# One clamp pass instead of two in a quantised feed-forward, with the scale handed to the gelu

## The chip, the cores and the metric

The kernel runs on one core of a Trainium2 chip. The metric is the device time of one execution in microseconds (us), lower is better. Five engines work beside each other, each with its own queue of instructions: TensorE (PE) for matmuls, VectorE (DVE), ScalarE (ACT), GpSimd (POOL) and SyncE (SP), which here only issues DMA transfers. They meet at semaphores: an instruction may wait for a count and raise one when it is done.

## The reference, cut to what matters

The model is a stack of small layers over 4096 tokens of 96 channels (16 images of 16 x 16): two convolution-like attention layers, a causal attention, a quantised feed-forward, a second causal attention and a mixture of four experts. The change is in the quantised feed-forward alone:

```
def _quantize_activations_groupwise(x):
    for g in range(NUM_GROUPS):                      # 5 groups along the batch
        ag = x[g * gs:(g + 1) * gs]
        gamma = jnp.max(jnp.abs(ag))
        xq[g] = clip(ag * QB / (gamma + EPS), -QB + EPS, QB - EPS)
def _bitlinear(x, W, b):
    y = einsum('btc,oc->bto', x, sign_binarised(W)) + b
    return _quantize_activations_groupwise(y)
h = _bitlinear(x, W1, b1)                            # 96 -> 384
h = jax.nn.gelu(h, approximate=False)
out = _bitlinear(h, W2, b2)                          # 384 -> 96
```

QB is 128 and EPS is 1e-5. Each group has one gamma, the largest magnitude over all its 768 tokens and all channels.

## The kernel before, in words

The layers run one after another on the one core, and nearly everything stays in SBUF. The order of every engine's work in this feed-forward is written by hand in three lists of steps (lines 76 to 78), one an engine. The digit of a step is its group of 768 tokens:

- TensorE, `F2_PE`: "h" is the first projection of a group, six pairs of matmuls into six PSUM buffers (L1035); "y" is the second projection, in two halves of 36 matmul records together (L1048).
- ScalarE, `F2_ACT`: "c" copies the six results of a group from PSUM into `big` (L652); "e" is the gelu of a whole group, in place (L656), 128 partitions by 3 x 768 elements. The gelu's activation table is loaded once, ahead of e0.
- VectorE, `F2_DVE`: "a" takes each partition's largest magnitude of a group (L1406); "q" quantises the group in place; "y" adds the bias to the second projection and takes its maximum (L1419, L1422); "f" quantises that, adds it to the residual and takes the token statistics (L1427, L1428, L1146, L1149).
- GpSimd makes the maximum over partitions of each "a" and "y" (L425).

So the lists begin on VectorE with a0, a1, q0, a2, q1, a3, q2, y0, a4, q3, y1, f0, q4, y2, f1, y3, and on TensorE with h0, h1, h2, h3, y0, h4, y1. On ScalarE the order is c0, c1, c2, e0, c3, e1, c4, e2, e3, e4. The second projection of group g starts when gelu g is done and VectorE has read the same half of the projection before. The third maximum and the later ones wait for the copies of their own group.

A step "q" starts with `quant_scale`: three one-column operations (L1398, L1399, L1400), each linked to the one before by a semaphore. They put gamma + EPS into column 2k+1 of `amax` and the scale QB / (gamma + EPS) into column 2k, the same number on all partitions. Then come two passes over the group: L1411 multiplies by the scale (a per-partition operand) and takes the minimum with a constant, L1412 takes the maximum with a constant. The gelu waits for the second.

After the feed-forward VectorE goes on to the layer norm (L1157 to L1165), whose output TensorE transposes (L706) for the next attention.

Of the kernel before, what the change touches and what calls it, by code (L numbers as in the profile page):

```python
# [9 lines left out]
ALU = mybir.AluOpType  # L10
ACT = mybir.ActivationFunctionType
# [5 lines left out]
P = 128  # L17
# [9 lines left out]
NG = 5  # L27
GI = B // NG
GT = GI * N
NE = 4  # L30
QB = 128.0
QEPS = 1e-5
# [52 lines left out]
def hybrid_kernel(nc, x_d, w96_d, w128_d, out_d):  # L85
    ctx = ExitStack()
    with ctx:
        def sb(name, shape, dt=F32):
            return ctx.enter_context(nc.sbuf_tensor(name, shape, dt))
# [3 lines left out]
        def sg(name):  # L93
            if name not in sems:
                sems[name] = ctx.enter_context(nc.semaphore(name))
            return sems[name]
# [59 lines left out]
        def wa(name, rows=P):  # L156
            a, b = C96[name]
            return w96[0:rows, a:b]

        def wb(name, rows=P):  # L160
            a, b = C128[name]
            return w128[0:rows, a:b]
# [31 lines left out]
        y1 = big[:, :].rearrange("p (j t) -> p j t", j=NJ)  # L194
# [11 lines left out]
        qk_f = qk[:, :, :, :, :].rearrange("p a h b x -> p (a h b x)")  # L206
        xhl = qk_f[:, 0:2048].rearrange("p (a b t) -> p a b t", a=2, b=2)
        amax = sb("amax", [P, 4, NG])
        gate = sb("gate", [P, 2, NT, NE])
        cmp = sb("cmp", [P, 6, NT])  # L210
        gsel = sb("gsel", [P, NE, NT])
# [231 lines left out]
        def _(act):  # L443
# [7 lines left out]
            def norm_tail(name):  # L451

                norm_sqrt(name, P, NT)
                act.wait_ge(sg("norm_scale"), TURN[name] // 8 + 1)
                for g in range(9):
                    if g < 8:
                        t = 4 * g + 3
                        nc.scalar.activation(on[:, t, :], tok[:, t, :], ACT.Identity, bias=st[:, 6, t:t + 1],
                                             scale=st[:, 5, t:t + 1]).then_inc(sg("ln_ta"), 1)
                    if g >= 1:  # L460
                        act.wait_ge(sg("ln_t_ps"), TURN[name] + g)
                        nc.scalar.activation(xn[0:C, (g - 1) * 512:g * 512], ps[0:C, 4 + (g - 1) % 4, :], ACT.Copy).then_inc(sg("xn_copied"), 1)
# [108 lines left out]
            for l in (1, 2, 3):  # L571
# [61 lines left out]
                if l == 2:  # L633

                    act.wait_ge(sg("f2_z"), 1)
                    for g in range(NG):
                        n = HID // NG
                        nc.scalar.activation(wa("f2_w1", C)[:, g * n:(g + 1) * n], wa("f2_w1", C)[:, g * n:(g + 1) * n], ACT.Sign,
                                             bias=s64[:, 1, g:g + 1]).then_inc(sg("f2_w1s"), 1)
                    for g in range(NG):  # L640
                        n = C // NG
                        v = wb("f2_w2").rearrange("p (j o) -> p j o", j=NJ)[:, :, g * n:(g + 1) * n]
                        nc.scalar.activation(v, v, ACT.Sign, bias=amax[:, 3, g:g + 1]).then_inc(sg("f2_w2s"), 1)
                    norm_tail("lnf2")
                    act.sem_inc(sg("f2_y1"), 6)
                    for step in F2_ACT:
                        g = int(step[1])
                        if step[0] == "c":
                            for b in range(2):
                                for j in range(NJ):  # L650
                                    act.wait_ge(sg("f2_y1_ps"), g * 6 + (b * NJ + j + 1))
                                    nc.scalar.activation(y1[:, j, g * GT + b * (GT // 2):g * GT + (b + 1) * (GT // 2)], ps[:, b * NJ + j, 0:GT // 2],  # L652
                                                         ACT.Copy).then_inc(sg("f2_y1"), 1)
                        else:
                            act.wait_ge(sg("f2_quant"), g + 1)
                            nc.scalar.activation(y1[:, :, g * GT:(g + 1) * GT], y1[:, :, g * GT:(g + 1) * GT], ACT.Gelu).then_inc(sg("f2_gelu"), 1)  # L656
            for g in range(8):
                act.wait_ge(sg("xres_ps"), g + 1)
                nc.scalar.activation(xc[:, g * 512:(g + 1) * 512], ps[0:C, g % 4, :], ACT.Copy).then_inc(sg("xres"), 1)
# [445 lines left out]
        def _(dve):  # L1105
# [3 lines left out]
            V = nc.vector  # L1109
            chain = [0]  # L1110

            def link(ins):

                chain[0] += 1
                ins.then_inc(sg("dve_chain"), 1)
                dve.wait_ge(sg("dve_chain"), chain[0])
# [176 lines left out]
            for l in (1, 2, 3):  # L1293
# [83 lines left out]
                if l == 2:  # L1377

                    n1, n2 = HID // NG, C // NG
                    V.tensor_reduce(out=s64[:, 0, 0:NG], in_=wa("f2_w1", C)[:, 0:NG * n1].rearrange("p (g o) -> p g o", g=NG), axis=AX.X, op=ALU.add).then_inc(sg("f2_wsum"), 1)  # L1380
                    w2v = wb("f2_w2").rearrange("p (j o) -> p j o", j=NJ)
                    for j in range(NJ):
                        last = V.tensor_reduce(out=cmp[:, j, 0:NG], in_=w2v[:, j, 0:NG * n2].rearrange("p (g o) -> p g o", g=NG), axis=AX.X, op=ALU.add)
                    link(last)
                    V.tensor_reduce(out=amax[:, 2, :], in_=cmp[:, 0:NJ, 0:NG].rearrange("p j g -> p g j"), axis=AX.X, op=ALU.add).then_inc(sg("f2_wsum"), 1)
                    dve.wait_ge(sg("f2_wtot"), 1)
                    V.tensor_scalar(s64[:, 1, 0:NG], ps[0:C, 0, 0:NG], -1.0 / (n1 * C), None, ALU.mult)
                    V.tensor_scalar(amax[:, 3, :], ps[:, 1, 0:NG], -1.0 / (n2 * HID), None, ALU.mult).then_inc(sg("f2_z"), 1)

                    V.memset(wa("f2_w1", C)[:, NG * n1:HID], 0.0).then_inc(sg("f2_w1z"), 1)  # L1390
                    V.memset(w2v[:, :, NG * n2:C], 0.0).then_inc(sg("f2_w2z"), 1)
                    layer_norm("lnf2")

                    def quant_scale(k, g):

                        dve.wait_ge(sg(f"f2_gmax{k}"), g + 1)
                        m, q = amax[:, 2 * k + 1, g:g + 1], amax[:, 2 * k, g:g + 1]
                        link(V.tensor_scalar(m, m, QEPS, None, ALU.add))  # L1398
                        link(V.reciprocal(q, m))  # L1399
                        link(V.tensor_scalar(q, q, QB, None, ALU.mult))  # L1400

                    for step in F2_DVE:
                        what, g = step[0], int(step[1])
                        if what == "a":
                            dve.wait_ge(sg("f2_y1"), g * 6 + 12)
                            V.tensor_reduce(out=amax[:, 0, g:g + 1], in_=y1[:, :, g * GT:(g + 1) * GT], axis=AX.XY, op=ALU.max,  # L1406
                                            apply_absolute_value=True).then_inc(sg("f2_amax0"), 1)
                        elif what == "q":
                            quant_scale(0, g)
                            v = y1[:, :, g * GT:(g + 1) * GT]  # L1410
                            link(V.tensor_scalar(v, v, amax[:, 0, g:g + 1], QB - QEPS, ALU.mult, ALU.min))  # L1411
                            V.tensor_scalar(v, v, -QB + QEPS, None, ALU.max).then_inc(sg("f2_quant"), 1)  # L1412
                        elif what == "y":
                            if g == 0:
                                dve.wait_ge(sg("f2_w2s"), NG)
                            for b in range(2):
                                dve.wait_ge(sg("f2_y2_ps"), 2 * g + b + 1)
                                t0 = g * 6 + b * 3
                                V.tensor_tensor(y2[:, t0:t0 + 3, :], ps[:, 6 + b, 0:3 * C].rearrange("p (t c) -> p t c", c=C),  # L1419
                                                mid_dim(wb("f2_b2"), 1, 3), ALU.add).then_inc(sg("f2_y2"), 1)  # L1420
                            dve.wait_ge(sg("f2_y2"), 2 * g + 2)
                            V.tensor_reduce(out=amax[:, 2, g:g + 1], in_=y2[:, g * 6:(g + 1) * 6, :], axis=AX.XY, op=ALU.max,  # L1422
                                            apply_absolute_value=True).then_inc(sg("f2_amax1"), 1)
                        else:
                            quant_scale(1, g)
                            v, tv = y2[:, g * 6:(g + 1) * 6, :], tok[:, g * 6:(g + 1) * 6, :]
                            link(V.tensor_scalar(v, v, amax[:, 2, g:g + 1], QB - QEPS, ALU.mult, ALU.min))  # L1427
                            link(V.scalar_tensor_tensor(out=tv, in0=v, scalar=-QB + QEPS, in1=tv, op0=ALU.max, op1=ALU.add))  # L1428
                            link(token_stats(range(6 * g, 6 * g + 6 if g < NG - 1 else NT)))
# [131 lines left out]
```

## Time and profile before

| | us |
|---|---|
| median of three runs | 922.02 |
| lowest and highest | 921.21 and 923.03 |
| profiled execution | 921.3 |
| its span, first to last instruction | 919.5 |
| TensorE busy | 796.1 (87%) |
| VectorE busy | 613.9 (67%) |
| ScalarE busy | 573.9 (62%) |
| GpSimd busy | 231.2 (25%) |

The mean granted clock of TensorE over the span is 0.923 of full speed. The feed-forward's work on the groups lies between some 509 and 574 us of the span. The busy shares are averages over stages with different limits, so they don't tell which engine bounds one stage: that is read from the chain that ended last, which is followed back from the last instruction to whatever released each step, and from the timelines of the stage. A row of a timeline merges equal instructions that follow each other; the bracket at its end is how long the engine was idle before it, and who released it.

### The profile page before, as it was taken

How to read it: one execution, taken by the hardware profiler on the slowest of the kernel's cores; microseconds unless marked ns; L12 is line 12 of the kernel's file. 1: busy time of each engine (PE TensorE's matmuls, PEld its weight loads, DVE VectorE, ACT ScalarE, POOL GpSimd, SP SyncE). 2: the span in 40 equal slices, each digit the busy share in tenths (PEclk: the TensorE clock that was granted, in tenths of full speed). 3: DMA queues.
4: the chain of work that ended last, by engine and by line, in shares of the span. 5: the costliest groups of instructions: out<-in, count | busy, mean ns of one | idle time of the engine just before them, and what ended most of it. 6: DMA issues, size and time to landing. Idle time of an engine off the chain costs nothing.

```text
span 919.5 us, 17419 instructions
## 1 busy us (share of the span) xinstructions
PE 796.1 (87%) x5452; PEld 606.3 (66%) x5452; DVE 613.9 (67%) x1584; ACT 573.9 (62%) x1341; POOL 231.2 (25%) x443
## 2 busy tenths in 40 slices
PE   0866799999999889999993874489999978999997
PEld 0852477878777867777772564257777758777775
DVE  6325677676668255777777599367677773677876
ACT  0202377777777356878884731467888754788875
POOL 9000336655553560000000000200000000234344
PEclk9998699999999698999996987789999985999999
DMA  5000001011111122333330000133333310231230
GB/s 191 1 0 1 0 2 14 16 17 18 18 19 18 26 70 71 99 89 86 103 94 9 1 1 0 44 88 86 92 103 87 87 33 3 69 86 44 57 74 17
DMA packets 63267, 44.42 MB, mean 48 GB/s; under 512 B 34416, under 2 KB 55280, under 8 KB 63088
## 3 DMA queue, kind: packets, MB, share of 16 engines
q1 hardware_dynamic: 63216, 43.78, 18.7%
q8 instruction: 27, 0.44, 0.2%
q14 instruction: 24, 0.20, 0.1%
HBM read 12.24 MB, written 3.21 MB: 17 GB/s over the span
## 4 chain that ended last, share of the span: by engine, by line
PE 75%; DVE 14%; issue 3%; ACT 2%; DMA 2%; POOL 2%; SPq 2%; POOLq 0%; DVEq 0%; ACTq 0%
PE ps L933 12%; PE ps L772 9%; PE ps L835 9%; PE ps L1085 7%; PE ps L1074 7%; PE ps L779 5%; PE ps L783 3%; PE ps L791 3%; PE ps L792 2%; PE ps L804 2%; PE ps L813 2%; DVE xn L1140 2%; DVE chst L1146 2%; PE ps L827 2%; SPq L242 2%
## 5 line engine op out<-in xcount | busy, mean ns | idle before, releaser
L502 ACT ACTIVATE ee<-ps,nmax 128x128 f32<-128x128 f32 (+1 forms) x584 | 207.9, 445 | 12.7 <-DVE nmax L1226 9.0
L933 PE MATMUL ps<-w,ee 128*128 128x128 f32 x960 | 140.9, 275 | 3.1 <-ACT big L489 0.9
L1226 DVE TENSOR_REDUCE nmax<-ps 128x2 f32<-128x256 f32 x200 | 101.8, 551 | 52.9 <-PE ps L783 52.9
L933 PEld LDWEIGHTS ps<-w,ee 128*128 128x128 f32 x960 | 111.6, 142 | 24.3 <-ACT ee L502 8.9
L489 ACT ACTIVATE big<-ps 128x512 f32<-128x512 f32 (+1 forms) x192 | 99.2, 546 | 24.6 <-PE ps L933 20.5
L1488 DVE TENSOR_TENSOR hhl<-ee,hhl 128x512 fp32r<-128x512 f32 x96 | 79.8, 837 | 32.2 <-ACT hhl L680 30.6
L1223 DVE TENSOR_REDUCE nmax<-ps 128x4 f32<-128x1024 f32 x48 | 58.8, 1225 | 58.8 <-PE ps L772 58.8
L772 PE MATMUL ps<-kh,big 128*128 128x256 f32 x384 | 93.8, 388 | 1.2 <-ACT ee L502 1.2
L835 PE MATMUL ps<-big,vh 128*32 128x256 f32 (+1 forms) x1188 | 92.2, 353 | 0.0
L306 POOL COPY xb<-xn 96x256 f32 (+1 forms) x52 | 20.6, 399 | 277.0 <-PE ps L804 248.1
L436 POOL TENSOR_TENSOR xc<-big,xc 96x512 f32<-96x512 f32 x32 | 52.6, 1643 | 135.9 <-DVE big L1482 135.7
L1074 PE MATMUL ps<-qk,w1hl 128*128 128x512 f32 x288 | 85.1, 407 | 0.4 <-DVE ee L1491 0.4
L1085 PE MATMUL ps<-hhl,w2hl 128*96 128x512 f32 x288 | 83.5, 399 | 0.3 <-DVE hhl L1488 0.3
L772 PEld LDWEIGHTS ps<-kh,big 128*128 128x128 f32 x384 | 71.4, 193 | 16.9 <-ACT ee L502 6.9
L1320 DVE COPY big<-ps 128x384 f32<-128x384 f32 x96 | 52.8, 550 | 38.8 <-PE ps L933 38.8
L677 ACT ACTIVATE ee<-ps 128x512 f32<-128x512 f32 x96 | 57.7, 601 | 30.5 <-PE ps L1074 30.5
L312 POOL TENSOR_TENSOR big<-qs,w 96x256 f32<-96x256 f32 x96 | 55.8, 613 | 70.6 <-ACT qs L511 70.6
L1341 DVE BATCH_NORM_STATS2 est<-ee 128x6 f32<-128x256 f32 x192 | 66.9, 411 | 0.0
L1074 PEld LDWEIGHTS ps<-qk,w1hl 128*128 128x128 f32 x288 | 55.9, 195 | 16.6 <-DVE ee L1491 0.7
L835 PEld LDWEIGHTS ps<-big,vh 128*32 128x32 f32 x1188 | 39.9, 110 | 39.9 <-issue 21.8
L779 PE MATMUL ps<-qk 64*128 64x128 f32 (+1 forms) x400 | 50.7, 332 | 10.7 <-DMA qk<-hl 7.7
L1085 PEld LDWEIGHTS ps<-hhl,w2hl 128*96 128x96 f32 x288 | 47.0, 164 | 18.9 <-issue 1.3
(241 smaller groups left out, 1339.0 us busy)
## 6 DMA issues: line engine op xcount, KB each, us to landing
qk<-hl SPq DMA_DIRECT2D x288, 96.0 KB, 3.1
big<-moe_gate SPq DMA_DIRECT2D x8, 768.0 KB, 6.7
w<-w_in SPq DMA_DIRECT2D x1, 1735.5 KB, 12.6
xc<-x_in SPq DMA_DIRECT2D x4, 384.0 KB, 5.6
l_mix<-on SPq DMA_DIRECT2D x32, 48.0 KB, 2.0
tok<-l_mix SPq DMA_DIRECT2D x16, 96.0 KB, 2.0
out<-xc SPq DMA_DIRECT2D x8, 192.0 KB, 2.1
w<-w_in SPq DMA_DIRECT2D x1, 998.0 KB, 9.0
```

What stands on the lines that cost most here:

```text
L489: nc.scalar.activation(et[:, h, 0:w], ps[:, 4 + hh, 0:w], ACT.Copy).then_inc(own(l, f"et{hh}"), 1)
L502: last = nc.scalar.activation(ee[:, ke, hh, qc, 0:w], src, ACT.Exp, bias=nmax[:, kp, hh, qc:qc + 1])
L772: last = mm(ps[:, 2 * kp + hh, qc * N:(qc + 1) * N], qh[:, par, 2 * u + hh, qc * P:(qc + 1) * P], kh[:, par, :], start=True, stop=True)
L779: mm(ps[:, 2 * kp + hh, qc * N:qc * N + w], qk[r0:r0 + 4 * HD, par, u, 0, qc * P:(qc + 1) * P], qk[r0:r0 + 4 * HD, par, u, 1, 0:w], start= ...
L835: last = mm(ps[32 * r:32 * (r + 1), 6, g * N + q0:(g + 1) * N], vh[:, par, tc, 3 * g + r, :], et[:, 3 * g + r, tc * N:tc * N + N - q0], st ...
L933: last = nc.tensor.transpose(ps[:, 4 + hh, b * P:(b + 1) * P], ee[:, u, hh, qc, tc * P:(tc + 1) * P], ident)
L1074: last = mm(ps[:, 4 + n % 4, :], w1hl[:, w, s * P:(s + 1) * P], xhl[:, t % 2, x, :], start=(k == 0), stop=(k == 2))
L1085: last = mm(ps[0:C, e, :], w2hl[:, w, s * C:(s + 1) * C], hhl[:, n % 4, h, :], start=(j == 0 and k == 0), stop=(j == NJ - 1 and k == 2))
L1223: last = V.tensor_reduce(out=nmax[:, kp, :, :].rearrange("p h q -> p (h q)"), in_=src, axis=AX.X, op=ALU.max, negate=True)
L1226: last = V.tensor_reduce(out=nmax[:, kp, :, qc], in_=ps[:, 2 * kp:2 * kp + 2, qc * N:qc * N + scores_cols(l, qc)], axis=AX.X, op=ALU.max, ...
L1341: last = V.bn_stats(est[:, par, q, 2 * u + hh, :], ee[:, u, hh, q, :])
L1488: V.tensor_tensor(hhl[:, n % 4, 1, :], hf[:, n % 4, :], hhl[:, n % 4, 0, :].bitcast(F32), ALU.subtract).then_inc(sg("moe_lo"), 1)
```

## The change

The clamp of step "q" becomes one pass. Clamping v times s to plus or minus (QB - EPS) is the same as clamping v to that bound divided by s, and multiplying afterwards. Since s is QB / (gamma + EPS), the bound on v is (gamma + EPS) (QB - EPS) / QB, which is computed in `amax`'s column 1 by a one-column multiplication; a second one writes its negative into a new one-column tile `bound`. The one large pass then takes the minimum with the first and the maximum with the second, both as per-partition operands. The multiplication by s moves into the gelu of ScalarE, which takes s as its per-partition scale operand. The two small operations are linked by the semaphore, as the three before them are.

```
@@ buffers
         amax = sb("amax", [P, 4, NG])
+        bound = sb("bound", [P, NG])
@@ ScalarE, step e
                             act.wait_ge(sg("f2_quant"), g + 1)
-                            nc.scalar.activation(y1[:, :, g * GT:(g + 1) * GT], y1[:, :, g * GT:(g + 1) * GT], ACT.Gelu).then_inc(sg("f2_gelu"), 1)
+                            nc.scalar.activation(y1[:, :, g * GT:(g + 1) * GT], y1[:, :, g * GT:(g + 1) * GT], ACT.Gelu,
+                                                 scale=amax[:, 0, g:g + 1]).then_inc(sg("f2_gelu"), 1)
@@ VectorE, step q
                             quant_scale(0, g)
+                            top, low = amax[:, 1, g:g + 1], bound[:, g:g + 1]
+                            link(V.tensor_scalar(top, top, (QB - QEPS) / QB, None, ALU.mult))
+                            link(V.tensor_scalar(low, top, -1.0, None, ALU.mult))
                             v = y1[:, :, g * GT:(g + 1) * GT]
-                            link(V.tensor_scalar(v, v, amax[:, 0, g:g + 1], QB - QEPS, ALU.mult, ALU.min))
-                            V.tensor_scalar(v, v, -QB + QEPS, None, ALU.max).then_inc(sg("f2_quant"), 1)
+                            V.tensor_scalar(v, v, top, low, ALU.min, ALU.max).then_inc(sg("f2_quant"), 1)
```

VectorE's order before, from the first two maxima through step q0 to the third maximum (`big` holds the group, 3 x 768 elements a partition; the bracket names the semaphore waited for):

```order
433 L1406 TENSOR_REDUCE amax<-big 128x1 [waits f2_y1] x2
434 L1398 TENSOR_SCALAR amax<-amax 128x1 [waits f2_gmax0]
435 L1399 RECIPROCAL amax<-amax 128x1 [waits dve_chain]
436 L1400 TENSOR_SCALAR amax<-amax 128x1 [waits dve_chain]
437 L1411 TENSOR_SCALAR big<-big,amax 128x3x768 [waits dve_chain]
438 L1412 TENSOR_SCALAR big<-big 128x3x768 [waits dve_chain]
439 L1406 TENSOR_REDUCE amax<-big 128x1 [waits f2_y1]
```

The same place now (lines stand two lower on VectorE and one lower on ScalarE):

```order
433 L1408 TENSOR_REDUCE amax<-big 128x1 [waits f2_y1] x2
434 L1400 TENSOR_SCALAR amax<-amax 128x1 [waits f2_gmax0]
435 L1401 RECIPROCAL amax<-amax 128x1 [waits dve_chain]
436 L1402 TENSOR_SCALAR amax<-amax 128x1 [waits dve_chain]
437 L1413 TENSOR_SCALAR amax<-amax 128x1 [waits dve_chain]
438 L1414 TENSOR_SCALAR bound<-amax 128x1 [waits dve_chain]
439 L1416 TENSOR_SCALAR big<-big,amax,bound 128x3x768 [waits dve_chain]
440 L1408 TENSOR_REDUCE amax<-big 128x1 [waits f2_y1]
```

Two one-column operations stand where the first large pass stood, the second large pass has two operands more, and nothing else has moved. On ScalarE the order stays; this is its piece around the first gelu now:

```order
368 L653 ACTIVATE big<-ps 128x384 [waits f2_y1_ps] x18
369 L657 ACT_TABLE_LOAD
370 L657 ACTIVATE big<-big,amax 128x3x768 [waits f2_quant]
371 L653 ACTIVATE big<-ps 128x384 [waits f2_y1_ps] x6
372 L657 ACTIVATE big<-big,amax 128x3x768 [waits f2_quant]
373 L653 ACTIVATE big<-ps 128x384 [waits f2_y1_ps] x6
```

Only the operand `amax` has come to the gelu.

## Rows read from the trace of the kernel before

**Rows 1.** The page: the chain that ended last, by engine, share of span.

```profile
PE 75%; DVE 14%; issue 3%; ACT 2%; DMA 2%; POOL 2%; SPq 2%; POOLq 0%; DVEq 0%; ACTq 0%
```

**Rows 2.** The chain, 490 to 600 us: start us, us, what.

```profile
555.00 5.87 PE ps L1048 x36
...
560.89 0.47 DVE on L1419
```

**Rows 3.** Waits, 505 to 575 us: waiting <- awaited: us in total, times, longest.

```profile
ACT big L656 <- DVE big L1412: 18.8, 5, 7.0
...
DVE on L1419 <- PE ps L1048: 1.0, 1, 1.0
```

**Rows 4.** Timeline of VectorE, 505 to 580 us: start us, us, instruction, idle before.

```profile
517.53 2.55 DVE L1406 TENSOR_REDUCE amax<-big 128x1 f32<-128x2304 f32 x1 [1.32 <-ACT big L652]
520.00 0.14 DVE L1398 TENSOR_SCALAR amax<-amax 128x1 f32<-128x1 f32 x1
520.18 0.16 DVE L1399 RECIPROCAL amax<-amax 128x1 f32<-128x1 f32 x1
520.38 0.15 DVE L1400 TENSOR_SCALAR amax<-amax 128x1 f32<-128x1 f32 x1
520.57 1.82 DVE L1411 TENSOR_SCALAR big<-big,amax 128x2304 f32<-128x2304 f32 x1
522.42 1.76 DVE L1412 TENSOR_SCALAR big<-big 128x2304 f32<-128x2304 f32 x1
524.10 2.54 DVE L1406 TENSOR_REDUCE amax<-big 128x1 f32<-128x2304 f32 x1
...
527.11 1.82 DVE L1411 TENSOR_SCALAR big<-big,amax 128x2304 f32<-128x2304 f32 x1
...
537.19 0.81 DVE L1419 TENSOR_TENSOR on<-ps,w 128x288 f32<-128x288 f32 x2
...
545.25 0.81 DVE L1419 TENSOR_TENSOR on<-ps,w 128x288 f32<-128x288 f32 x2
...
554.41 0.81 DVE L1419 TENSOR_TENSOR on<-ps,w 128x288 f32<-128x288 f32 x2
```

**Rows 5.** Timeline of ScalarE in the same stretch.

```profile
521.39 1.28 ACT L656 ACT_TABLE_LOAD   x1
524.21 2.12 ACT L656 ACTIVATE big<-big 128x2304 f32<-128x2304 f32 x1 [1.54 <-DVE big L1412]
526.24 2.38 ACT L652 ACTIVATE big<-ps 128x384 f32<-128x384 f32 x6
...
532.79 2.38 ACT L652 ACTIVATE big<-ps 128x384 f32<-128x384 f32 x6
```

**Rows 6.** Timeline of TensorE there; below, its busy us and granted clock (PEclk).

```profile
526.48 4.23 PE L1048 MATMUL ps<-w,big 128*128 128x96 f32 x36 [1.77 <-ACT big L656]
530.55 4.06 PE L1035 MATMUL ps<-xn,w 128*128 128x384 f32 x12
537.77 5.86 PE L1048 MATMUL ps<-w,big 128*128 128x96 f32 x36 [3.16 <-DVE on L1419]
...
540.00:542.00 2.00, 2.00 (x11) 0.50 0.00 0
```

**Rows 7.** Lines L1307, L1140, L1165, L458: ns min/median/max, starts, forms.

```profile
L1307 DVE TENSOR_SCALAR w<-w x2: 200/206/211, 101.1 to 581.5; 128x96 f32<-128x96 f32 x2
...
L1140 DVE TENSOR_SCALAR xn<-xc,st x32: 394/404/4109, 15.0 to 98.3; 96x256 f32<-96x256 f32 x32
...
L1165 DVE TENSOR_SCALAR on<-tok,st x72: 320/325/334, 499.0 to 758.2; 128x96 f32<-128x96 f32 x72
...
L458 ACT ACTIVATE on<-tok,st x24: 450/454/467, 499.0 to 765.6; 128x96 f32<-128x96 f32 x24
```

**Rows 8.** Timeline of ScalarE, 750 to 785 us, at another table load.

```profile
774.16 1.28 ACT L677 ACT_TABLE_LOAD   x1
775.45 0.60 ACT L677 ACTIVATE ee<-ps 128x512 f32<-128x512 f32 x1
```

## The prediction

> **What bounds the kernel now.** I read the chain that ended last first, then the waits of the stretch that the change touches, then its timelines engine by engine. Over the whole span the chain lies on TensorE for 75% and on VectorE for 14% [rows 1], so most of the 919.5 us can't gain from an edit of VectorE. In the quantised feed-forward it is the other way round. From 517.5 us, where the second maximum (step a1) stops waiting for ScalarE, the chain runs through VectorE alone until 555 us, where it goes once to TensorE and comes back at 560.89 [rows 2]. The waits say the same: ScalarE waits 18.8 us for the clamp's last pass, and VectorE waits for TensorE only once, 1.0 us, ahead of an L1419 [rows 3]. So what leaves VectorE between 520 and 554 us leaves the span, as long as nobody else comes late. After 554 us the order of work is unchanged and moves as one block: VectorE feeds the last two projections, then the statistics, then the layer norm, on which everything later waits.
>
> **The block that changes.** One step "q" on VectorE is three linked one-column operations (start to start 0.18, 0.20 and 0.19 us), then L1411 (1.82 us, multiply by the scale and clamp above), then L1412 (1.76 us, clamp below). L1411 starts at 520.57, L1412 at 522.42, and the next maximum at 524.10 [rows 4]: 3.53 us from the first large pass to the next step. There are five such steps, one a group.
>
> *Removed:* both large passes, 3.53 us a step.
>
> *Added, the one large pass.* It reads two per-partition bounds; no row has that form at this size. What a per-partition operand costs: L1307, 128x96 with a constant alone, takes 206 ns; L1165, the same shape with two per-partition operands, 325 ns [rows 7]. So two of them cost 119 ns. L1411 has one and takes 61 ns more than L1412, which fits. That the two don't slow the rate is seen between 96 and 256 columns: 325 and 404 ns, 0.49 ns a column [rows 7], no more than the 0.76 of L1412 (1758 ns for 2304). So I take 1.76 + 0.12 = 1.88 us. The next maximum needs no result of it and starts before it has ended: 524.10 against the end of L1412 at 522.42 + 1.76 = 524.18, an overlap of 0.08. Start to start: 1.80 us. The low end would be one operand's price, as L1411's 1.82 (1.74 start to start). The high end is the rate of the maximum over the same elements, 2.54 us [rows 4], plus 0.12: 2.66, or 2.58 start to start. I take 1.80, since the shape and pass are those of L1412 and both two-operand rows lie on the fast side.
>
> *Added, two one-column operations*, each waiting for the one before. They are of the kind of L1398 and L1400, 0.18 to 0.20 start to start [rows 4]; 0.37 together, and nothing hides them, as they are ahead of the large pass. Between 0.30 (their own durations with nothing between) and 0.40.
>
> Saved a step: 3.53 - 1.80 - 0.37 = 1.36 us; five steps: **6.8 us**. The ends: with 1.74 and 0.36, 1.43 a step, 7.1; with 2.58, 0.58 a step, 2.9.
>
> *Added, the scale on the gelu.* ScalarE reads one per-partition operand more. L458, 96 columns with two of them, takes 454 ns [rows 7]; at the gelu's 2.12 us for 2304 columns [rows 5] 96 of them are at most 0.09, so an operand costs between nothing and 0.18 us. I take 0.1, the middle: the gelu becomes 2.22 us, between 2.12 and 2.30. It is paid beside VectorE's work. The cover is checked next.
>
> **Does everybody else keep up?** I walk the new times. q0: its three small operations are at 520.00 as before; the pass starts at 520.57 + 0.37 = 520.94 and ends at 522.82.
> - *Gelu 0.* The activation table is loaded from 521.39 to 522.67 [rows 5], so it is ready 0.15 us before the data. The gelu starts at 522.85 (before: 524.21) and ends at 525.07. The six copies of group 3 took 2.38 us and started 0.09 before the gelu's end [rows 5]; now they end at about 527.4. The maximum a3 wants them when VectorE has done q1: a2 starts at 522.74, its q1 pass 3.01 + 0.37 later (524.10 to 527.11 before [rows 4]) at 526.12, a3 at 527.92. Cover 0.5 us.
> - *Projection 0 and the matmuls of group 4.* They followed the gelu by 0.15 us and lasted until 534.61 [rows 6]; now 1.26 earlier, 533.35, and the last copy of group 4 is done half a microsecond behind, at about 533.9 (ScalarE, with gelu 1 done at 530.2, has caught up by then). VectorE reaches y0 at 537.19 - 3 x 1.36 = 533.10 and a4 1.51 us later (8.06 between y0 and y1, less 3.02 and 3.53), 534.6. Cover 0.7.
> - *Projection 1* began 0.58 after y0 and took 5.86 us [rows 4, 6]: from 533.7 to 539.5. VectorE takes its first half at 545.25 - 4 x 1.36 = 539.8. Its cover shrinks from 1.6 to 0.3, and the half read first is done well before.
> - *Projection 2* starts behind y1's first half, at 540.4, and is done at 546.2; y2 is reached at 554.41 - 6.8 = 547.6. Cover 1.4. From there all is as before, the 1.0 us wait too.
>
> TensorE's clock matters here. Projection 0 took 4.23 us with the clock granted in full (2.4 GHz); projection 1, at 0.50 (1.2 GHz) for a part (540 to 542 [rows 6]), took 5.86 after a pause. One such stretch is worth 1.63 us. In y3 (5.87 us, also one stretch) it is what makes VectorE wait: without it 1.0 us more is gained, with a second one 1.6 lost. The change moves the work against these stretches, and I can't tell which way: it goes into the range.
>
> Here a rule of the Trainium skill speaks against the change. The row first: behind the table load of 774.16, 1.28 us long, the activation starts at 775.45, 0.01 us after its end [rows 8]; behind the one at 521.39 nothing shows it, because the gelu waits for VectorE until 524.21 anyway. The skill's page "ScalarE: Activation LUTs", section "What ACT_TABLE_LOAD costs", gives a switch of tables a drain of about 1.38 us beside the 1.28 us load. If that stood behind the load, the sum would be 6.1 instead of 6.8 (an estimate from that figure, by the way of rival 2); by the row it is 6.8, and I go by the row.
>
> **The sum.** The profiled execution took 921.3 us (919.5 in the span, 1.8 around it); less 6.8 is 914.5. The median of the runs is 922.02, 0.7 above it, so the predicted time is 922.0 - 6.8 = 915.2.
>
> **Rivals.**
> 1. *The two-bound pass runs one element at a time*, at the maximum's rate. 2.9 us saved: 919.1. For: no row has the form at 3 x 768. Against: the two-operand rows of 96 and 256 columns. 8%.
> 2. *ScalarE becomes the bound at group 3.* If the first gelu can't start sooner than it did, at 524.21, because ScalarE needs until then after its table load, it ends at 526.4, the copies of group 3 at 528.7, and a3 waits 0.8 us (528.7 against 527.9). Projection 0 and the copies of group 4 then end where they did, 535.2, against a4 at 535.4: they just hold. 6.0 saved: 916.0. The skill's section on the table load speaks for it. For: only 0.15 us between load and data. Against: the activation at 775.45 [rows 8]. 10%.
> 3. *Slower.* The clamp with both bounds taken from operands is issued as two turns over the elements, each at the maximum's rate: 5.1 us, 5.0 start to start. Then a step costs 5.0 + 0.37 - 3.53 = 1.84 more, 9.2 in all: 931.2. It turns slower once the pass is over 3.16 us start to start (3.53 - 0.37), 1.4 ns an element. For: minimum and maximum with two operands stand in no row. Against: L1411 and L1412 have the same rate whatever they compute. 3%.
> 4. *No change*: the gain is taken back by TensorE, as stretches at the lower clock in the layer norms and attentions that follow. It would take four stretches of 1.63 more than before, and rows show no reason why they should all fall on one side. 3%.
>
> **How the numbers follow.** My forecast has 76%, with a range of its own of 913.2 to 917.8: 7.8 or 7.1 saved at one end and 5.2 (a second stretch) at the other, and a microsecond around the median, as the three runs lie between 921.21 and 923.03. For 8 in 10 I give 912.8 to 918.4, which takes in rival 2 and leaves out rivals 1, 3 and 4. About 0.2% (1.8 us) is what a measurement of this kernel can tell from no change: faster 76 + 10 + 8 = 94, less 1 for rival 1's 919.1 lying near that bound: 93%; the same 3 + 1 = 4%; slower 3%.
>
> **What the profile after would show.** One large pass of about 1.88 us, five of them, and the next maximum 1.80 us after its start; two more one-column operations, 0.37 us a step. Large pass to next maximum and back: 5.2 us instead of 6.54 in the first three groups. Gelus of 2.2 us, the first starting at 522.85. VectorE idle between the first maximum and the layer norm still about 1 us, in y3 alone. The second half of y3 6.8 us earlier than 560.89. A pass of 2.6 us or more, a gelu starting at 524, a wait of the fourth maximum for ScalarE, or a wait at y1 for TensorE would each show a step wrong.

## The result, and the profile after

| | us | ratio to before, 95% |
|---|---|---|
| before, median | 922.27 | |
| changed kernel, median of four runs (913.94 to 915.72) | 915.15 | 0.9922 (0.9905 to 0.9939) |
| predicted | 915.2 | |

7.1 us faster, where 6.8 were forecast. Timed again beside the experiments, the changed kernel took 915.74, a ratio of 0.9929 (0.9917 to 0.9942).

The timeline of VectorE after, over step q0 and into the third maximum, has these rows (start us, us, instruction, idle before); lines stand two lower than before:

```profile
519.78 2.55 DVE L1408 TENSOR_REDUCE amax<-big 128x1 f32<-128x2304 f32 x1 [1.32 <-ACT big L653]
522.25 0.14 DVE L1400 TENSOR_SCALAR amax<-amax 128x1 f32<-128x1 f32 x1
...
522.62 0.15 DVE L1402 TENSOR_SCALAR amax<-amax 128x1 f32<-128x1 f32 x1
522.81 0.15 DVE L1413 TENSOR_SCALAR amax<-amax 128x1 f32<-128x1 f32 x1
523.00 0.15 DVE L1414 TENSOR_SCALAR bound<-amax 128x1 f32<-128x1 f32 x1
523.19 1.88 DVE L1416 TENSOR_SCALAR big<-big,amax,bound 128x2304 f32<-128x2304 f32 x1
524.99 2.54 DVE L1408 TENSOR_REDUCE amax<-big 128x1 f32<-128x2304 f32 x1
...
528.38 1.88 DVE L1416 TENSOR_SCALAR big<-big,amax,bound 128x2304 f32<-128x2304 f32 x1
...
556.36 0.46 DVE L1423 TENSOR_TENSOR on<-ps,w 128x288 f32<-128x288 f32 x1 [0.96 <-PE ps L1050]
...
570.15 0.18 DVE L1159 TENSOR_SCALAR st<-chmv 128x32 f32<-128x32 f32 x1
```

Beside [rows 4]: the pass takes 1.88 us and the next maximum starts 1.80 after it (3.53 before for the two), the two new operations take 0.19 each, and from pass to pass it is 5.19 us instead of 6.54. The last row is the layer norm's first operation behind the feed-forward. In the timeline of before it is this one:

```profile
574.68 0.18 DVE L1157 TENSOR_SCALAR st<-chmv 128x32 f32<-128x32 f32 x1
```

I use the distance from the second maximum to this row as the length of the stretch. It is 57.15 us before (517.53 to 574.68) and 50.37 after (519.78 to 570.15): 6.78 us less. That is the forecast, instruction by instruction. From here on "the stretch" is this distance, and "the rest" is the span without it.

The span fell by 5.6 us (919.5 to 913.9), not by 6.8, because the rest of the kernel, which is untouched, differs between executions: 2.25 us more ahead of the stretch, 1.07 less behind it. About 0.6 us of the first arises between 80 and 112 us of the span, where TensorE's clock was lower. These are the windows of TensorE's busy us (with its instructions) and granted clock, first before, then after:

```profile
80.00:108.00 28.00, 14.26 (x38) 0.63 0.00 1
```

```profile
80.00:108.00 28.00, 14.23 (x34) 0.57 0.00 1
```

In the executions before, after and in c0, e1, e2, e3, e6, e8, e9 and e10 the rest took between 861.5 and 865.0 us, with nearly nothing edited there. So one execution's span can't show a microsecond. The stretch can, as it came out at 50.37 or 50.38 in the three executions in which its work was the same (after, c0, e10); but it too moves by a microsecond or two when TensorE's lower clock falls on another of its matmuls, as e4 shows below, so it has to be read with its waits.

Who waits for whom in the stretch after (505 to 570 us):

```profile
ACT big L657 <- DVE big L1416: 10.4, 4, 5.6
...
DVE on L1423 <- PE ps L1050: 1.0, 1, 1.0
...
PE ps L1050 <- ACT big L657: 0.5, 1, 0.5
```

Beside [rows 3]: ScalarE's wait for VectorE fell from 18.8 to 10.4 us, and VectorE still waits only for the one half of projection 3. The chain that ended last crosses to TensorE at the same place as in [rows 2]:

```profile
550.46 5.87 PE ps L1050 x36
```

ScalarE after, to be read beside [rows 5]:

```profile
523.63 1.28 ACT L657 ACT_TABLE_LOAD   x1
525.10 2.22 ACT L657 ACTIVATE big<-big,amax 128x2304 f32<-128x2304 f32 x1 [0.19 <-DVE big L1416]
527.23 2.37 ACT L653 ACTIVATE big<-ps 128x384 f32<-128x384 f32 x6
```

The gelu went from 2.12 to 2.22 us by its scale operand. It waited 0.19 us for the data behind the table load, so the load did not delay it. The copies of group 3 end at 529.60, 0.58 ahead of the maximum a3 at 530.18: such a lead of a result over the instruction that asks for it is called its cover here.

TensorE after, beside [rows 6]:

```profile
531.53 4.06 PE L1037 MATMUL ps<-xn,w 128*128 128x384 f32 x12
535.95 4.23 PE L1050 MATMUL ps<-w,big 128*128 128x96 f32 x36 [0.36 <-DVE on L1423]
```

Projection 1 now begins 0.36 us behind the matmuls of group 4 instead of 3.16, its clock stays granted in full, and it takes 4.23 us instead of 5.86; so does projection 2 (at 542.66, before at 545.84). The 1.63 us are worth nothing in either place: projection 1 is done at 540.18, and VectorE reads it after step q3, at 542.07; projection 2 is done at 546.89 and read at 549.87.

### The profile page after: what moved, and what is told of

Its sections match the earlier page's. It is cut to its first block, busy times and chain, and to the rows that moved or that the text cites. A ratio compares the mean times of both kernels' runs of the same rounds, so it can differ in the third digit from the quotient of the medians.

```text
span 913.9 us, 17424 instructions
## 1 busy us (share of the span) xinstructions
PE 794.6 (87%) x5452; PEld 604.3 (66%) x5452; DVE 607.7 (66%) x1589; ACT 575.0 (63%) x1341; POOL 230.4 (25%) x443
## 3 DMA queue, kind: packets, MB, share of 16 engines
q1 hardware_dynamic: 63216, 43.78, 18.8%
## 4 chain that ended last, share of the span: by engine, by line
PE 77%; DVE 14%; issue 3%; ACT 2%; POOL 2%; DMA 2%; SPq 1%; POOLq 0%; DVEq 0%; ACTq 0%
PE ps L935 12%; PE ps L774 9%; PE ps L837 9%; PE ps L1087 7%; PE ps L1076 7%; PE ps L781 5%; PE ps L785 4%; PE ps L793 3%; PE ps L794 2%; PE ps L806 2%; PE ps L815 2%; DVE xn L1142 2%; DVE chst L1148 2%; PE ps L829 2%; PE ps L729 1%
```

## The experiments

The stretch is the one defined above, in the one profiled execution of each kernel. Each ratio is to the kernel before as timed beside that experiment, with its 95% interval.

| kernel | median us | ratio to before, 95% | stretch us |
|---|---|---|---|
| before | 922.3 | | 57.15 |
| c0, changed kernel again | 915.74 | 0.9929 (0.9917 to 0.9942) | 50.38 |
| e1, two passes with the two bounds | 926.40 | 1.0037 (1.0025 to 1.0050) | 60.53 |
| e2, pass over even halves | 914.84 | 0.9914 (0.9901 to 0.9927) | 47.64 |
| e3, small operations side by side | 912.47 | 0.9893 (0.9878 to 0.9908) | 47.01 |
| e4, early table, one run | 920.54 | | 51.98 |
| e5, e2 + e3 + e4 | 915.98 | 0.9937 (0.9919 to 0.9955) | 46.23 |
| e6, idle copy ahead of gelu 0 | 918.38 | 0.9964 (0.9951 to 0.9977) | 53.76 |
| e7, e5 in a new order | 917.69 | 0.9954 (0.9938 to 0.9969) | 50.49 |
| e8, e2 + e3, table behind the hand-over | 910.96 | 0.9884 (0.9866 to 0.9901) | 46.22 |
| e9, e2 + e3 | 912.70 | 0.9897 (0.9882 to 0.9913) | 46.79 |
| e10, the changed kernel with the table load as in e8, one run | 913.67 | | 50.37 |

### c0 and e1: is it the second pass, and nothing else?

> The changed kernel once more, as the mark for the other three. Every theory: 915.2 us, the ratio to the kernel before at 0.992 to 0.993.

> As the changed kernel (bounds made by two small operations, scale in the gelu), but the minimum and the maximum in two large passes again, each with one per-partition bound. My theory (the gain is the length of one pass on VectorE's chain, nothing else): passes of 1.82 us, 1.85 + 1.74 from the first pass to the next step in place of 1.80, so 1.79 x 5 = 9.0 us more than the changed kernel, 924.1 us, 0.2% slower than the kernel before, since the two small operations are then paid for nothing. Rival (the gain comes from taking the multiplication away from VectorE, or from the new times at which TensorE works): 915 to 918 us.

```diff
-    V.tensor_scalar(v, v, top, low, ALU.min, ALU.max).then_inc(sg("f2_quant"), 1)
+    link(V.tensor_scalar(v, v, top, None, ALU.min))
+    V.tensor_scalar(v, v, low, None, ALU.max).then_inc(sg("f2_quant"), 1)
```

926.4 us, slower than the kernel before by 0.25 to 0.50%. VectorE's groups in the stretch (busy us, mean ns, idle before):

```profile
L1424 DVE TENSOR_TENSOR on<-ps,w 128x288 f32<-128x288 f32 x10 | 4.2, 448 | 2.2 <-PE ps L1050 2.1
...
L1417 DVE TENSOR_SCALAR big<-big,bound 128x2304 f32<-128x2304 f32 x5 | 9.1, 1819 | 0.2
L1416 DVE TENSOR_SCALAR big<-big,amax 128x2304 f32<-128x2304 f32 x5 | 9.1, 1818 | 0.2
```

The stretch is 10.15 us longer than in c0: 9.0 for the passes, as expected, and 1.2 because the wait for projection 3 grew from 0.97 to 2.15. The time missed the expected one by 2.3 us: 1.2 is that wait, and in the profiled execution the rest was 1.7 longer than in c0. The rival, that the gain came with the multiplication's move to ScalarE, is refuted: that move is in this kernel, and the gain isn't. Against the kernel before the stretch is 3.4 us longer: 1.9 for the small operations, 0.3 for the operand that the second pass has more, and 1.2 of the wait.

### e2: what sets the rate of the pass?

> As the changed kernel, but the one large pass goes over the same 2304 elements as 2 x 3 x 384 instead of 3 x 768. Theory A (two elements at a time are had only when the outer dimension can be halved, and three rows are run as two turns of 768: 1877 ns is 277 of fixed cost and 1600 for 1536): the pass takes 1.48 us, 0.40 less. Five of them would be 2.0 us; ScalarE's table load ends only 0.19 us before the first gelu, so the copies of group 4 come late by some 0.2 to 0.3 and 1.7 us are saved: 913.4 us. Theory B (the rate of 0.7 ns an element is that of the memory, whatever the shape): 915.2 us, the pass 1.88 us as before. A loss (a pass of 2.6 us, 918.8) if a three-dimensional pattern goes one element at a time.

```diff
+    v = v.rearrange("p j (h t) -> p h j t", h=2)
     V.tensor_scalar(v, v, top, low, ALU.min, ALU.max).then_inc(sg("f2_quant"), 1)
```

The line of the pass in e2 (ns min/median/max, starts, forms):

```profile
L1417 DVE TENSOR_SCALAR big<-big,amax,bound x5: 1478/1478/1480, 523.7 to 547.3; 128x2304 f32<-128x2304 f32 x5
```

1478 ns, the 1.48 us of theory A, for the same elements at the same addresses. Theory B is refuted. The stretch fell by 2.74 us, 1 more than expected: 5 x 0.40, and the wait for projection 3 (1.0) is gone because TensorE's low-clock part fell on projection 2 (5.86 us) instead, less 0.3 of new waits ahead of a3 and a4. That last microsecond is no merit of the pass. The medians differ by 0.9 us (1.7 expected) and the intervals overlap: the time alone would not have decided it.

Behind the table load, with no wait left, the gelu starts at once:

```profile
524.13 1.28 ACT L657 ACT_TABLE_LOAD   x1
525.42 2.22 ACT L657 ACTIVATE big<-big,amax 128x2304 f32<-128x2304 f32 x1
```

### e3: what do five one-column operations cost?

> As the changed kernel, but each step q makes (gamma + eps) / QB and both bounds straight from gamma in three small operations that don't wait for each other, and the reciprocal stands behind them beside the large pass: four small operations with one exposed wait instead of five with five. Step f gets two linked small operations instead of three. Theory (a linked one-column operation costs 0.19 us for the wait on its result, an unlinked one about 0.07): a step q shorter by about 0.5 us and a step f by 0.19, 2.5 + 0.95 = 3.4 us, less some 0.5 of new waits of the maxima a3 and a4 for ScalarE's copies: 912.2 us. Rival (the cost is that of the instruction, not of the link): only one operation less in q and one in f, 0.19 x 10 = 1.9 us, 913.3 us.

```diff
+    V.tensor_scalar(unit, m, QEPS, 1.0 / QB, ALU.add, ALU.mult)
+    V.tensor_scalar(top, m, QEPS, (QB - QEPS) / QB, ALU.add, ALU.mult)
+    link(V.tensor_scalar(low, m, QEPS, (QEPS - QB) / QB, ALU.add, ALU.mult))
+    V.reciprocal(q, unit)
     V.tensor_scalar(v, v, top, low, ALU.min, ALU.max).then_inc(sg("f2_quant"), 1)
```

VectorE's timeline of e3 in q0 and at the two maxima:

```profile
521.45 0.14 DVE L1413 TENSOR_SCALAR bound<-amax 128x1 f32<-128x1 f32 x1
521.51 0.14 DVE L1414 TENSOR_SCALAR bound<-amax 128x1 f32<-128x1 f32 x1
521.57 0.14 DVE L1415 TENSOR_SCALAR bound<-amax 128x1 f32<-128x1 f32 x1
521.75 0.16 DVE L1416 RECIPROCAL amax<-bound 128x1 f32<-128x1 f32 x1
521.83 1.86 DVE L1418 TENSOR_SCALAR big<-big,bound 128x2304 f32<-128x2304 f32 x1
...
528.65 2.55 DVE L1407 TENSOR_REDUCE amax<-big 128x1 f32<-128x2304 f32 x1 [0.35 <-ACT big L653]
...
535.17 2.55 DVE L1407 TENSOR_REDUCE amax<-big 128x1 f32<-128x2304 f32 x1 [0.31 <-ACT big L653]
```

Unlinked operations start 0.06 us apart, linked ones 0.18. The small part of a step q fell from 0.94 to 0.38 us (0.56 less), where one operation less would have given 0.19; a step f fell by 0.19. Ten steps give 3.75 us. Of that a3 and a4 take back 0.66, as they now wait for ScalarE's copies, and 0.4 comes from TensorE's waits (0.60 us at projection 2 in place of 0.97 at projection 3, as the lower clock fell elsewhere). Against c0 that is 3.3 us of time and 3.4 of stretch; the rival's 1.9 is too little.

### e4, e10 and e6: the table load and the cover of the first gelu

> As the changed kernel, but the gelu's table is loaded right behind the layer norm, while ScalarE waits for the first projection anyway. My theory (in the changed kernel the load ends 0.19 us before the data is there, so it costs nothing): the stretch from the second maximum to the layer norm behind the feed-forward stays at 50.4 us, the whole at 915 to 916. Rival (the switch holds the engine beyond its 1.28 us, and the first gelu was late): the stretch gets shorter by up to 1 us.

```diff
                     norm_tail("lnf2")
+                    nc.scalar.preload_act_table_set("gelu_and_others")
                     act.sem_inc(sg("f2_y1"), 6)
```

The stretch grew by 1.6 us, and the gelu isn't the reason, as no maximum behind it waits for ScalarE: TensorE's rows of e4 show the last two projections at 11.46 us instead of 9.88, with more of them at the lower clock. Why the clock fell there in this one execution isn't shown. The start of the second maximum was late too, at 521.85, and 1.4 us of this is my edit's fault. The load stands ahead of the semaphore that hands TensorE its PSUM buffers, so TensorE's first wait is 2.08 us instead of 0.68:

```profile
513.31 15.72 PE L1038 MATMUL ps<-xn,w 128*128 128x384 f32 x48 [2.08 <-ACT L646]
...
552.55 11.46 PE L1051 MATMUL ps<-w,big 128*128 128x96 f32 x72 [1.95 <-DVE on L1424]
```

So e4 doesn't answer its question. e10 does, with the two lines exchanged:

> As the changed kernel, with the table load behind the hand-over of the PSUM buffers as in e8, and nothing else. Theory (the load never held up the changed kernel): start of the second maximum, stretch behind it (50.4 us) and time (915 to 916) as in the changed kernel, give or take one stretch of TensorE's lower clock, 1.6 us. Rival (the load hides a delay of the first gelu): stretch under 50.

```profile
522.71 2.21 ACT L658 ACTIVATE big<-big,amax 128x2304 f32<-128x2304 f32 x1 [1.49 <-DVE big L1417]
```

The gelu waits 1.49 us for VectorE, and the stretch is 50.37 us, the same as with the load in front of the gelu. So the load held up nothing in the changed kernel. The second maximum started at 517.38, 1.6 us earlier than in c0, though I had expected it at the same place; TensorE's wait ahead of its first matmuls is 0.68 us in both, so this comes from the layers ahead and is not the load's doing.

> As the changed kernel, with one idle copy of 1152 elements a partition (weights into an unused tile, some 1.1 us) on ScalarE between the wait for q0 and the first gelu: it takes away the cover that the gelu had. Theory (copies of group 3 were done 0.6 us before the maximum a3 asked for them, copies of group 4 0.7 before a4): a3 now waits 0.5 us, and everything behind is 0.5 us later, 915.9 us; stretch 50.9 us instead of 50.4. Rival A (ScalarE has slack everywhere): stretch 50.4. Rival B (ScalarE is on the chain): the whole 1.1 us, 51.5.

```diff
     act.wait_ge(sg("f2_quant"), g + 1)
+    if g == 0:
+        nc.scalar.activation(ee_f[:, 0:1152], wb("f3_w2")[:, 0:1152], ACT.Copy)
```

```profile
523.27 1.16 ACT L658 ACTIVATE ee<-w 128x1152 f32<-128x1152 f32 x1 [1.48 <-DVE big L1418]
524.44 1.28 ACT L659 ACT_TABLE_LOAD   x1
525.74 2.22 ACT L659 ACTIVATE big<-big,amax 128x2304 f32<-128x2304 f32 x1
...
534.67 0.49 ACT L653 ACTIVATE big<-ps 128x384 f32<-128x384 f32 x1 [2.33 <-PE ps L1039]
```

```profile
528.10 5.86 PE L1052 MATMUL ps<-w,big 128*128 128x96 f32 x36 [2.97 <-ACT big L659]
```

```profile
530.27 2.55 DVE L1410 TENSOR_REDUCE amax<-big 128x1 f32<-128x2304 f32 x1 [1.84 <-ACT big L653]
...
538.42 2.55 DVE L1410 TENSOR_REDUCE amax<-big 128x1 f32<-128x2304 f32 x1 [1.35 <-ACT big L653]
```

The first block is ScalarE's timeline, the second TensorE's, the third VectorE's. The copy pushed the table load behind it too, so the first gelu came 2.5 us late, not 1.1, and all three expected numbers are wrong. The cover can still be read: 2.5 late, a3 waits 1.84, so 0.6 were covered, as the trace after had said. The maximum a4 then waits 1.35 more, and this is TensorE's clock: behind an idle time of 2.97 us projection 0 took 5.86 us instead of 4.23 (the granted clock was 0.50 from 530 to 532), and the matmuls of group 4 stand behind it. Without these 1.63 us the last copy of group 4 would have been there by the time of a4. Together the two waits are 3.2 of the 3.4 us by which the stretch grew.

### e5, e8 and e9: both improvements together

> The even halves of e2, the small operations of e3 and the early table of e4 together. If all added up from e3's stretch of 47.0 us: 5 x 0.39 less for the pass. But the matmuls of group 4 stand behind projection 0, which can't start before the matmuls of group 3 are done, so the fourth group's copies come only 0.3 us earlier and the maximum a4 waits for them by 1.5 us or so. Theory (TensorE's order is the new limit in the first half): stretch 46.0 us, 911.4 us. Rival (VectorE stays the limit): 45.0 us, 910.4 us.

The stretch was near the expected 46.0, at 46.23, though its waits were others: a4 waits 0.93 us and not 1.5, a3 0.34, and projection 3 is waited for by 1.15. The time missed by 4.6 us. 1.4 is e4's fault (TensorE waits 2.08 us ahead of the stretch), and in the profiled execution 1.66 more went into the first matmuls, 17.41 us instead of 15.75, partly at a lower clock. e4 has the same wait without these 1.66, so they don't follow from it. The remainder isn't explained.

> As e5, but the table load stands behind the semaphore with which ScalarE hands TensorE its first six PSUM buffers, not ahead of it. In e5 and e4 TensorE waited 2.08 us for that load before its first projection, 1.4 us more than the 0.68 of the changed kernel. Theory: that wait is back at 0.7, the stretch from the second maximum to the layer norm stays at 46.2 us, and the time is 1.4 us under e5's and 0.8 under e3's: 911.7 us. Rival (the load ahead of the first copies costs its time in any place): 912.8 us or more.

> As e8, but with the table load where it was, ahead of the first gelu. Theory (gelu 0 starts 0.7 us later than VectorE is done with q0, and TensorE has nothing to do until then, so projection 0 and all behind it up to the maximum a4 come 0.3 us later than in e8): stretch 46.5 us, 912.0 us. Rival (0.3 us is covered elsewhere): the same as e8.

VectorE's timeline of e8, its three waits behind the second maximum:

```profile
526.91 2.55 DVE L1408 TENSOR_REDUCE amax<-big 128x1 f32<-128x2304 f32 x1 [0.34 <-ACT big L654]
533.66 2.55 DVE L1408 TENSOR_REDUCE amax<-big 128x1 f32<-128x2304 f32 x1 [0.93 <-ACT big L654]
551.02 0.46 DVE L1427 TENSOR_TENSOR on<-ps,w 128x288 f32<-128x288 f32 x1 [1.16 <-PE ps L1051]
```

and TensorE's first matmuls:

```profile
509.46 15.75 PE L1038 MATMUL ps<-xn,w 128*128 128x384 f32 x48 [0.68 <-ACT xn L463]
```

The wait is back at 0.68, and e8 has the lowest median of the case: 910.96 us, 1.16% under the kernel before. Against e9 it gains 0.57 us of stretch (0.3 expected): there a3 waits 1.15 us instead of 0.34, since the late gelu delays the copies of group 3, which I had left out, and a4 0.69 instead of 0.93. The intervals of e8, e9 and e3 overlap, so their times don't rank them.

### e7: a new order that was no better

> As e5, with the three lists of steps in another order: TensorE makes the first projection of group 4 ahead of the second projection of group 0, ScalarE copies it ahead of gelu 1, and VectorE goes a3, q2, a4, q3, y0, q4, f0, y1, f1, y2, f2, y3, y4, f3, f4. Theory (what was left were waits for TensorE and ScalarE set by the order): VectorE works through from the second maximum on; its own work is about 44 us, so stretch 44.3 us, 909.7 us. Rival (the maximum over partitions on GpSimd, now only 1.8 us ahead of f0, or projections y2 and y3 one behind the other, hold it up instead): no shorter than e5.

```profile
DVE on L1427 <- PE ps L1051: 5.0, 4, 2.2
...
DVE amax L1401 <- POOL amax L426: 1.0, 2, 0.5
```

The stretch is 50.49 us where I had expected 44.3. My theory fell and the rival stands: VectorE now waits 5.0 us in four places for TensorE's second projections and 1.0 us for GpSimd's maxima. With y0 moved behind q3, TensorE gets its second projections in two bunches of two behind pauses (11.02 and 11.46 us), partly at the lower clock. The old order had spread them under steps q and f. How much of the 5.0 us is the order and how much the clock isn't separated.

## Why the prediction was right

- *The chain.* The stretch ran on VectorE, so what left it left the span. e1 puts one pass back and loses more than the change saved.
- *The pass*, forecast at 1.88 us from two rows of 96 and 256 columns: measured 1.877. Rivals 1 and 3 (2.66 and 5.1 us) were wrong. One reading behind it was too quick. The 0.49 ns that a column costs between 96 and 256 was set against 0.76 for L1412, whose 0.76 holds its fixed cost too, and taken to say only that two operands don't slow the rate. They don't, but it also said that a pass of another shape is faster, which was left unasked and which e2 shows.
- *The two small operations*, forecast 0.37 us, measured 0.38. The forecast gave 0.30 as their low end and then worked out the end of the sum with 0.36; with 0.30 it is some 7.4 us saved instead of 7.1, which changes nothing here.
- *The gelu's operand*, forecast 0.1 us, measured 0.09, and off the chain. Had its cover of 0.6 been used up, e6 shows the price.
- *The covers.* The forecast had 0.5 us at a3 (0.58 measured), 0.7 at a4 (0.75) and the first gelu 0.15 behind the table load (0.19). Rival 2 was wrong here: e2 and e3 remove the slack, and the gelu starts 0.01 us after the load. The Trainium skill ("ScalarE: Activation LUTs", "What ACT_TABLE_LOAD costs") gives a switch of tables a drain of about 1.38 us beside the load; no such time is seen behind a load in this kernel. In e2 and e3, and not in the change itself, the load is what the gelu waits for.
- *TensorE's clock.* The wait ahead of y3's second half stayed at 0.96 us (0.97 in c0 and e10), so the range's term for it (1.0 more, 1.6 less) wasn't drawn. The forecast had no reason for this, so it is luck. It was a fair term: e2 gained it, and e1 and e4 lost to it. The walk had projections 1 and 2 at 5.86 us with parts at the lower clock, and both took 4.23; that was wrong and harmless, as both have cover. Rival 4, more low clock in the layers behind, didn't come: the time behind the stretch was 1.07 us shorter.
- *Where luck helped.* The sum gives a time only up to the rest of the kernel, which lay anywhere in some 3.5 us in the profiled executions; 915.15 and, timed again, 915.74 against 915.2 is closer than the method is.

What I didn't see: that the pass itself could be had in 1478 ns instead of 1877 by another shape, and that linking cost more than the instruction that e3 does without (0.37 against 0.19 us of the 0.56 saved a step).

## What to carry to other kernels

Find the engine of the chain in the stretch that is edited, not in the whole; where it is one engine working through, a pass taken off it is worth its start-to-start length, and the operand it gains and the small operations that feed it can be priced from rows with the same kind of operands, and its rate from a pass of the same shape. Then walk the new times through the other engines: the covers at a3 and a4 were 0.58 and 0.75 us here, and the next two improvements already ran into them. Judge edits of a microsecond by the stretch in the trace and by its waits, and look at which matmuls the lower clock fell on. Put a table load behind a semaphore that another engine waits for: ahead of it, it cost 1.4 us here.

## What the runs showed of the hardware

- The VectorE pass with two per-partition bounds takes 1877 ns over 3 x 768 elements, and 1478 over 2 x 3 x 384 of the same elements. The numbers fit two rows at a time: three rows are two turns of 768, which is 1536 steps, and the halves are one turn of 1152. The 399 ns between them for 384 steps are 0.96 steps a nanosecond, which leaves some 280 ns of fixed cost. Two shapes can't test a rule with two unknowns, so this is an inference; for it speaks that the 1.48 us was worked out ahead of the run. The Trainium skill, "VectorE: DVE Perf Modes", "Mode 2×_2P — use both read ports for one tensor", says that the outermost dimension is split in half between the ports, and allows an odd one if source and destination have the same.
- Each per-partition operand costs such a pass some 60 ns (1758, 1819, 1877 with none, one, two over 3 x 768) and the gelu 92 (2124 to 2216). One or two arithmetic steps in a pass make no difference: with one operand it is 1819 for two steps (L1411 before) and 1818 or 1819 for one (e1).
- Dependent one-column operations, linked by a semaphore, start 0.18 to 0.20 us apart, independent ones 0.06 (e3).
- TensorE's granted clock fell to 0.50 in different places of the same work from one kernel to the next, at 1.0 to 1.6 us each where something waited (e1, e2, e4, e6), and nothing where nobody did.
